# Attention scores and their maxima three head groups ahead instead of two, with a six-slot ring of separated keys

## The reference, cut to what matters

```python
q = split_heads(query @ Wq + bq); k = split_heads(key @ Wk + bk); v = split_heads(value @ Wv + bv)
scores = einsum('bhqd,bhkd->bhqk', q, k) / sqrt(8)
scores = where(mask[:, None] == 0, -1e9, scores)
p_attn = softmax(scores, axis=-1)
x = einsum('bhqk,bhkd->bhqd', p_attn, v)
x = x.transpose(0, 2, 1, 3).reshape(B, T, 128) @ Wo + bo
```

## Time and profile before

| | us |
|---|---|
| median of 3 runs (256.17 to 257.1) | 256.29 |
| the profiled execution's own time | 254.04 |
| span of the profiled execution | 252.2 |
| TensorE busy in it | 192.8 (76%) |
| VectorE busy | 191.0 (76%) |
| ScalarE busy | 135.0 (54%) |
| GpSimd busy | 113.6 (45%) |
| attention: first and last start of an exponential (L740) | 119.9 and 189.0 |

### The profile page before, as it was taken

The page is one execution under the profiler, slowest core; times in us unless marked ns, Lnnn a source line. Parts: engine busy times, 40 slices in busy tenths (PEclk is TensorE's granted clock), DMA queues, the critical chain, the costliest instruction groups (busy, mean ns, idle before and its releaser), DMA issues.

```text
span 252.2 us, 4609 instructions
## 1 busy us (share of the span) xinstructions
PE 192.8 (76%) x1654; PEld 126.8 (50%) x1654; DVE 191.0 (76%) x459; ACT 135.0 (54%) x271; POOL 113.6 (45%) x228
## 2 busy tenths in 40 slices
PE   0269576799846668776989988988878987999950
PEld 0158555589732157663433543534546864666420
DVE  1998696898784997969866786886665439499996
ACT  2215841393968559544867567767793554431000
POOL 6690453855554938860587784784140020000000
PEclk9999995789995679999999999999999999999995
DMA  6994030000000000000000000000000000000000
GB/s 169 345 405 169 0 127 39 4 0 4 0 4 0 0 0 3 0 5 0 3 0 5 0 1 3 0 3 0 3 1 3 0 3 1 0 3 21 21 21 21
DMA packets 4460, 8.73 MB, mean 35 GB/s; under 512 B 514, under 2 KB 3026, under 8 KB 4052
## 3 DMA queue, kind: packets, MB, share of 16 engines
q1 hardware_dynamic: 3636, 7.78, 8.8%
q10 hardware_dynamic: 800, 0.63, 0.8%
HBM read 7.88 MB, written 0.52 MB: 33 GB/s over the span
## 4 chain that ended last, share of the span: by engine, by line
PE 36%; DVE 27%; POOL 18%; issue 10%; ACT 7%; DMA 2%; ACTq 0%; POOLq 0%; DVEq 0%
PE ps L1193 32%; POOL gate_pt L515 6%; PE ps L1202 4%; POOL rstd L377 3%; POOL w L397 3%; DVE rden L888 3%; DVE mx L1046 2%; DVE stats L780 2%; DVE gate_pt L989 2%; DMA cst<-consts_dram 2%; DVE amax L983 2%; ACT gate_pt L740 2%; POOL spread L502 2%; DVE picksum L1158 2%; DVE emb L830 2%
## 5 line engine op out<-in xcount | busy, mean ns | idle before, releaser
L1046 DVE TENSOR_REDUCE mx<-ps 128x2 f32<-128x512 f32 x64 | 42.0, 686 | 15.2 <-PE ps L1193 15.1
L740 ACT ACTIVATE gate_pt<-ps 128x512 f32<-128x512 f32 x64 | 37.0, 603 | 15.2 <-PE ps L1193 14.9
L515 POOL TENSOR_SCALAR gate_pt<-ka 32x256 f16<-32x256 f16 x64 | 25.5, 399 | 4.4
L1193 PE MATMUL ps<-gate_pt,half_c 128*128 128x512 f16 x64 | 24.1, 379 | 2.8 <-DVE half_c L1036 1.5
L1193 PE MATMUL ps<-qb,gate_pt 128*128 128x256 f16 x128 | 24.6, 274 | 1.0 <-ACT gate_pt L740 0.2
L1193 PE MATMUL ps<-gate_pt,hid_xm 128*32 128x256 f32 x256 | 20.4, 390 | 1.5 <-ACT gate_pt L740 1.5
L1193 PE MATMUL ps<-w,half_c 128*128 128x512 f16 x96 | 21.2, 379 | 0.0
L1193 PEld LDWEIGHTS ps<-qb,gate_pt 128*128 128x128 f16 x128 | 9.1, 97 | 18.5 <-issue 10.6
L377 POOL TENSOR_TENSOR rstd<-vareps,halfs 128x2 f32<-128x2 f32 x24 | 17.2, 717 | 2.0
L1202 PE MATMUL ps<-cst,rows 128*128 128x128 f32 x32 | 7.9, 352 | 11.9 <-ACT rows L645 5.1
L502 POOL TENSOR_SCALAR spread<-mx 128x16 f16<-128x16 f32 x32 | 5.9, 201 | 23.4 <-DVE mx L1046 17.2
(11 more groups left out here) (221 smaller groups left out, 525.7 us busy)
## 6 DMA issues: line engine op xcount, KB each, us to landing
stage<-weights_dram SPq DMA_DIRECT2D x2, 1024.0 KB, 11.1
wf<-weights_dram SPq DMA_DIRECT2D x4, 256.0 KB, 8.3
wf<-mask_dram SPq DMA_DIRECT2D x1, 1024.0 KB, 4.7
eb_oT<-ffw_dram SPq DMA_DIRECT2D x1, 768.0 KB, 7.8
x_in<-x_dram SPq DMA_DIRECT2D x4, 128.0 KB, 2.9
ctx_in<-ctx_rows_dram ACTq DMA_DIRECT2D x4, 128.0 KB, 5.5
gate_pt<-ctx_cols_dram SPq DMA_DIRECT2D x1, 512.0 KB, 8.3
out_dram<-ctx_in SPq DMA_DIRECT2D x4, 128.0 KB, 1.7
```

Source lines behind the costliest of these rows:

```text
L515: ins = nc.gpsimd.tensor_scalar(kz[part, n % KRING, k], ka[part, b, quad], 1.0, 0.0, ALU.mult, ALU.add)
L740: nc_act(pt[:, head % PRING].rearrange("p t n -> p (t n)"), ps[:, 2 + head % 2, :], ACT.Exp, scale=DK ** -0.5).then_inc(sig["probs"], 1)
L1046: V.tensor_reduce(mx[:, b, head:head + 2, t], score_bank(4 * n + i).rearrange("p (h n) -> p h n", h=2), AX.X, ALU.max).then_inc(sig["smax" ...
L1193: return nc.tensor.matmul(dst, lhsT, rhs, start=start, stop=stop, skip_group_check=True)
```

## The change

A third quad of plain scores and maxima is put ahead of the shifted scores, on TensorE and VectorE. The ring of separated keys grows from four slots to six, the two new ones in a buffer of their own, cleared by a memset of their own. GpSimd fills six slots ahead of its loop: four before `shift_rows(0)`, two after `shift_rows(1)`. In its loop `shift_rows` stays at n + 2 and the keys go to n + 6. `shift(0)` stands in the middle of quad 2 instead of quad 1.

```diff
-KRING = 4
+KRING = 6
+KRING_LOW = 4
+LEAD = 3
@@ buffers
-        kz = taken(gate_pt, PRING * TILES * T, KRING * 4 * T // 2).bitcast(F16).rearrange(
-            "p (r h n) -> p r h n", r=KRING, h=4)
+        kz_low = taken(gate_pt, PRING * TILES * T, KRING_LOW * 4 * T // 2).bitcast(F16).rearrange(
+            "p (r h n) -> p r h n", r=KRING_LOW, h=4)
+        kz_high = sb("kz_high", [P, KRING - KRING_LOW, 4, T], F16)
+
+        def kz(n):
+
+            r = n % KRING
+            return kz_low[:, r] if r < KRING_LOW else kz_high[:, r - KRING_LOW]
@@ GpSimd
             pool.wait_ge(sig["kscale"], 1)
-            nc.gpsimd.memset(kz[:, :, :, :], 0.0).then_inc(sig["zeros_ready"], 1)
+            nc.gpsimd.memset(kz_high[:, :, :, :], 0.0)
+            nc.gpsimd.memset(kz_low[:, :, :, :], 0.0).then_inc(sig["zeros_ready"], 1)
             for b in range(B):
                 rstd_of(LN_ATT, b)
...
-                    ins = nc.gpsimd.tensor_scalar(kz[part, n % KRING, k], ka[part, b, quad], 1.0, 0.0, ALU.mult, ALU.add)
+                    ins = nc.gpsimd.tensor_scalar(kz(n)[part, k], ka[part, b, quad], 1.0, 0.0, ALU.mult, ALU.add)
...
-            for n in range(KRING):
+            for n in range(QUADS):
+                separated_keys(n)
+            pool.wait_ge(sig["kz_ready"], QUADS)
+            shift_rows(0)
+            shift_rows(1)
+            pool.wait_ge(sig["spread"], 2)
+            for n in range(QUADS, KRING):
                 separated_keys(n)
             pool.wait_ge(sig["kz_ready"], KRING)
-            shift_rows(0)
-            shift_rows(1)
@@ VectorE
-            for k in range(4):
-                head_max(1, k)
+            for n in range(1, LEAD):
+                for k in range(4):
+                    head_max(n, k)
...
-                    if n + 2 < B * QUADS:
-                        head_max(n + 2, k)
+                    if n + LEAD < B * QUADS:
+                        head_max(n + LEAD, k)
@@ TensorE
                 for k in range(4):
                     scores(1, k, masked)
+                for k in range(4):
+                    scores(2, k, masked)
                     if k == 1:
                         pe.wait_ge(sig["qa_ready"], B)
                         shift(0)
                 for n in range(B * QUADS):
                     for k in range(4):
                         shifted_scores(n, k, masked)
-                        if n + 2 < B * QUADS:
-                            scores(n + 2, k, masked)
+                        if n + LEAD < B * QUADS:
+                            scores(n + LEAD, k, masked)
```

More of the change, by code:

```diff
@@ L1406, in scores @@
                 ins = mm(dst, qa[:, b, quad, t * P:(t + 1) * P],
-                         kz[:, n % KRING, 2 * pair_of:2 * pair_of + 2].rearrange("p h n -> p (h n)"), True, not masked)
+                         kz(n)[:, 2 * pair_of:2 * pair_of + 2].rearrange("p h n -> p (h n)"), True, not masked)
                 if masked:
@@ L1433, in shifted_scores @@
                     dst = ps[:, 2 + head % 2, t * T:(t + 1) * T]
-                    ins = mm(dst, kz[:, n % KRING, k, tok], qb[:, n % 2], True, not masked)
+                    ins = mm(dst, kz(n)[:, k, tok], qb[:, n % 2], True, not masked)
                     if masked:
```

## The result

| | before | after |
|---|---|---|
| median of 17 runs each, us | 255.61 | 257.78 |
| lowest and highest | 253.87, 257.57 | 256.36, 259.97 |
| ratio, 95% interval | | 1.0092 [1.0067, 1.0116] |
| profiled execution: time, span | 254.04, 252.2 | 256.82, 255.0 |
| its mean granted clock | 0.942 | 0.925 |

The change makes the kernel slower by 0.9%, some 2.3 us. Ratios leave out executions more than 1.5% above a kernel's fastest. The forecast was 256.3, no change, with 254.8 to 258.3 as range: the time lies in the range, but the likeliest case did not come. That it lies in the range is luck in part. The forecast stood on 256.29, the median of three runs; with 17 runs the kernel before is at 255.61. As differences the forecast was +0.05 with -1.5 to +2.0 as range, and +2.2 to +2.3 was measured.

What follows compares the result with a forecast made beforehand. It took TensorE's order and the banks VectorE and ScalarE give back as the bound, with GpSimd only tying. Terms 2.5 + 0.65 - 0.85 - 1.25 - 1.0 = +0.05 on 256.29 gave 256.3 us, range 254.8 to 258.3.

Steps and rivals of the forecast that it cites:

- likeliest case: Base case for the whole kernel: the terms nearly cancel, +0.05 us, so 256.3 us; chance 0.50.
- What bounds: Attention quads: TensorE's order and the banks VectorE and ScalarE give back set 3.69 us; GpSimd only ties.
- fast rival: Quads 2 to 12: GpSimd bounds every quad, so the period falls to 3.47 us; -2.4 us, 253.9; chance 0.16.
- Start of the loop: Attention's start: shift(0) waits behind plain score (2,1) at VectorE's rate, so the first exponential comes later; +2.5 us.
- Memset: Before the layer norm's roots: clearing the two new slots on GpSimd delays them; +0.65 us, bounds 0 and 1.8.
- Separated keys: GpSimd in the attention: same count, keys 4 and 5 after shift_rows(1) still leave shift_rows in time; 0 us.
- Spread waits: Quads 2 and 3: TensorE's waits for spread go and both fall back to 3.69 us; -0.85 us.
- Tail step 4: ScalarE's rows: GpSimd makes the deviation earlier, ending the 0.62 us wait in batches 0 and 1; -1.25 us.
- Drain: Attention's end: quad 13 has no plain scores and the one-hot no longer meets a weight quarter; -1.0 us.
- Contention: Quad 8: GpSimd's weight quarter slows VectorE's one-hot of batch 0, TensorE waits; +1.1 us, 257.4; chance 0.20.
- Clock: Attention's start: thin work drops TensorE to 1.2 GHz, slowing quads 0 and 1; +3 us, 259.3; chance 0.06.
- The ends of the sum: All terms' bounds taken in one direction: about -3.1 and +3.4 us; a few together give +-0.9.

Runs made afterwards that it cites:

- e5: Changed kernel plus filler matmuls, results never read, where TensorE stood waiting before the row transposes and in quads 0 to 2; 256.89 us, ratio 1.0046 to the kernel before.
- e10: e8 plus the filler matmuls of e5; 255.53 us, ratio 0.9977 to the kernel before.
- e4: Kernel before plus only a second buffer that nothing reads and its memset ahead of the ring's; 257.71 us, ratio 1.0082 to the kernel before.
- e9: Changed kernel with the lead back at two quads, shift(0) in quad 1 and the memset early, ring of six kept; 256.30 us, ratio 1.0024 to the kernel before.
- e1: Changed kernel with the first quarter of m2 split by GpSimd in quad 7 instead of quad 8; 256.55 us, ratio 1.0053 to the kernel before.
- e2: Changed kernel with the memset of the two new slots moved ahead of the wait for gscale; 255.76 us, ratio 0.9989 to the kernel before.
- e8: Changed kernel with the memset early and the first quarter of m2 in quad 7; 255.14 us, ratio 0.9982 to the kernel before.
- e12: e8 measured a second time; 254.93 us, ratio 0.9965 to the kernel before.

## Why the prediction was right or wrong

- **What bounds.** Right. A quad with nothing late in it took 3.69 us before and takes it after (quads 1, 4 and 8), and those with a tail step but no late rows take 4.43 and 4.91 before, 4.43 and 4.90 after (quads 5 and 6). Ahead of the drain only the quads with a named wait became shorter. The fast rival, GpSimd as the bound of every quad, is dead, though the chain of waits seemed to carry it.
- **Start of the loop, +2.5.** Right at full clock: e5 and e10 have 2.6 more than before (7.61 and 7.62 for 5.00). In the changed kernel it is +3.23 - 0.20 = 3.0, and the 0.4 between is the clock's, TensorE being granted 0.50 from 122 to 124.
- **Memset, +0.65.** Measured 0.67 in its place. But the step passed on the delay alone and put at nothing what the delay does to the work behind it, and there it failed: in three of four profiled executions TensorE fell to 1.2 GHz in the projections. In e4 the memset costs 1.9 to 2.1 us, three times the term and past its upper bound of 1.8.
- **Separated keys, 0.** Right; no wait for `spread`. The margin was made by the lead, as e9 shows, where the ring alone has 3.3 us of such waits.
- **Spread waits, -0.85.** Measured -0.86.
- **Tail step 4, -1.25.** The wait of 0.62 went as forecast, and the two quads' groups gave -0.75 each, 1.5. Right, a little small.
- **Drain, -1.0.** Measured -1.0, with the one-hot at 0.37 and its quarter gone from there.
- **Contention, held at 0.20.** It came, priced at 1.1 and measured at +0.90: the one-hot went from 0.37 to 1.27, though the quarter started 0.07 us behind it. Taking it out of the base case was a choice on a coincidence of 0.01 us. The Trainium skill (GPSIMD Engine Reference, Specifications) says that GpSimd's SBUF interfaces are shared with VectorE, with contention for VectorE instructions in a 2-port mode or with two SBUF inputs. This trace agrees that they contend, 1.27 us for 0.37; which of the two kinds the one-hot is, no run here shows.
- **Clock, held at 0.06 and priced +3.** It came, in two places, at less. At the start of the attention, the only place where I considered it, it cost 0.4 us and not 3; the costlier fall was in the projections, behind the memset. The failing step is the comparison with the stretch at 116 to 118: one thin stretch that kept its clock in one execution was taken for a rule. The Trainium skill (Perfetto Trace Analysis, Matmul Optimizations) warns that TensorE's power follows its utilization. The changed kernel agrees, 0.50 after 0.89 of 2 us busy; e1 and e2, with 1.00 after 0.63, show that one row does not tell.
- **The ends of the sum.** The lower ends of the terms add to 2.0 + 0 - 1.6 - 1.4 - 1.4 = -2.4, not the -3.1 that was written; nothing rests on it.

So the sum of the lead's own terms was nearly exact. Forecast were 2.5 - 0.85 - 1.25 - 1.0 = -0.6; the attention in e10, at full clock, is 0.74 shorter than before, and in e8 and e12, with the fall at the start, 0.30 and 0.32. The two side effects that were kept as rivals both happened. As an outcome, slower by over 0.5% had only 0.24.

## What to carry to other kernels

Clear new buffers where an engine idles for another reason, not in front of work that others wait for; here moving one memset was worth nearly three times its visible delay. State a forecast as a difference, and be sure of its base: three runs had it 0.7 us too high. When a change slides one engine's work against another's, list the pairs that share a way to memory and look at what meets now. A chain of waits that ties is no bound: check whether the waiting engine had idle time before the step that is to be made earlier. To price one effect of under 1 us, take the length between two events around it in several profiles; here the loop's repeated within 0.02 us (63.66 four times, 64.56 to 64.58), where whole times scatter by some 3 us.

## What was not expected of the hardware

A delay of 0.67 us on GpSimd moved the mean granted clock of TensorE over all runs from 0.937 to 0.926 (e4), and TensorE then stood at 0.50 in stretches where it was busy all of 2 us. The clock is not fixed for a kernel: e8's twelve executions were granted 0.928 to 0.942, and the kernel before 0.929 to 0.947, so one profile does not tell whether a given thin stretch costs the clock. Fillers raised the changed kernel's mean from 0.921 to 0.939, above that of the kernel before, and still left it slower than e8 at 0.931: the mean clock by itself does not rank kernels.
